# A graph layer with attention, a mixer and eight experts: the first nodes of the expert stage prepared in the last attention step, and the expert loop written out

## The reference

```python
xn = layernorm(x)
gnn = relu(gat_conv(xn))          # softmax over each node's edges, 4 heads of 64:
                                  #   out[n] = sum_e exp(e)*xp[src] / sum_e exp(e)
qkv = xn @ W_qkv + b_qkv          # q, k centred; q2 = l2norm(q*q / (sum q*q + 1e-7)) per node
mix = (v + q2 @ kv / sqrt(N)) @ W_out + b_out
x = x + gnn + mix                 # "base" of a node below: x + v-part + scaled q-part + constant
z = layernorm(x)
w = softmax(mean_over_batch(z) @ Wr + br)            # 8 weights a node
for e in range(8):                                   # three 256x256 products each
    h = relu(bn(z @ W1[e] + b1[e])); h = relu(bn(h @ W2[e] + b2[e]))
    x += w[:, e] * (h @ Wo[e] + bo[e])
```

## Time and profile before

| quantity | value |
|---|---|
| median of 3 runs | 3340.61 us (3336.39 to 3344.05) |
| the profiled execution: its own time | 3340.92 us |
| the profiled execution: span | 3339.1 us |
| PE busy | 2875.5 us (86%) |
| DVE busy | 2209.1 us (66%) |
| ACT busy | 1550.5 us (46%) |
| POOL busy | 1505.3 us (45%) |
| mean granted TensorE clock | 0.867 of full speed |
| `experts` stage, first instruction to end of span | 2214.04 to 3339.1 us |

### The profile page before, as it was taken

How to read it: one execution, slowest core, us unless ns; L and a number is a source line. 1 busy time by engine, 2 the same in 40 slices (tenths; PEclk the granted TensorE clock), 3 DMA queues, 4 the chain that set the end, 5 groups by cost and what they waited for, 6 DMA issues and landing times. The chain is left out here.

```text
span 3339.1 us, 62774 instructions
## 1 busy us (share of the span) xinstructions
PE 2875.5 (86%) x18549; PEld 2173.3 (65%) x18549; DVE 2209.1 (66%) x6073; ACT 1550.5 (46%) x4109; POOL 1505.3 (45%) x1625
## 2 busy tenths in 40 slices
PE   5678887888887888888888888859999999999999
PEld 3567666667766776777777777745665656566655
DVE  5457787787887877887878888864444444545424
ACT  3245555555555565565565555533332333333332
POOL 0177777777777777777777777500000000000000
PEclk9777888887877888787788787869999999999999
DMA  7544444444444444444444444431001010101000
GB/s 245 171 138 121 126 121 121 123 124 123 124 115 114 125 129 125 128 122 124 128 127 127 126 124 123 101 128 34 22 24 45 1 45 0 45 1 45 1 12 11
DMA packets 163365, 316.34 MB, mean 95 GB/s; under 512 B 32208, under 2 KB 97360, under 8 KB 162896
## 3 DMA queue, kind: packets, MB, share of 16 engines
q0 software_dynamic: 75552, 212.96, 24.5%
q1 hardware_dynamic: 78576, 90.49, 8.5%
q10 hardware_dynamic: 8896, 8.82, 0.8%
HBM read 272.44 MB, written 39.70 MB: 93 GB/s over the span
## 5 line engine op out<-in xcount | busy, mean ns | idle before, releaser
L758 POOL DMA_INDIRECT xg<-edge_table,idx x1568 | 1490.3, 950 | 501.7 <-issue 485.3
L1024 PE MATMUL ps_y<-y,hotw 128*128 128x260 f32 x3520 | 909.3, 421 | 41.0 <-issue 37.9
L1024 PEld LDWEIGHTS ps_y<-y,hotw 128*128 128x128 f32 x3520 | 721.9, 212 | 201.1 <-issue 50.8
L1515 ACT ACTIVATE h<-ps_h,bnb,bns 128x448 f32<-128x448 f32 x448 | 324.1, 723 | 624.2 <-PE ps_h L1475 624.2
L1617 DVE SCALAR_TENSOR_TENSOR yb<-ps_ye,wts,yb 128x256 f32<-128x256 f32 x392 | 189.7, 484 | 576.0 <-PE ps_ye L1483 576.0
L891 ACT ACTIVATE y<-xg,w 128x65 f32 x1760 | 466.5, 338 | 7.4 <-ACT w L883 0.4
L1241 DVE TENSOR_TENSOR y<-xg,ps_v 128x780 f32<-128x780 f32 x440 | 418.1, 961 | 8.8
L940 ACT CAST hotw<-hot 128x512 f32<-128x512 bf16 x440 | 267.1, 622 | 272.8 <-PE ps_y L1024 271.8
L1475 PE MATMUL ps_h<-zt,w 128*128 128x448 f32 x896 | 362.3, 559 | 6.0 <-issue 5.7
L1483 PE MATMUL ps_ye<-wo,h 128*128 128x256 f32 x1568 | 348.1, 379 | 0.0
L1475 PE MATMUL ps_h<-h,w 128*128 128x448 f32 x896 | 345.9, 539 | 0.0
(11 more groups left out here) (231 smaller groups left out, 2880.5 us busy)
## 6 DMA issues: line engine op xcount, KB each, us to landing
xg<-edge_table,idx POOLq DMA_INDIRECT x1568
mix_rows<-kk SPq DMA_DIRECT2D x49, 257.0 KB
t<-mix_rows SPq DMA_DIRECT2D x7, 1799.0 KB, 7.6
xb<-xn_turned SPq DMA_DIRECT2D x50, 128.0 KB
x<-in_x SPq DMA_DIRECT2D x7, 896.0 KB, 8.0
xn_rows<-xn SPq DMA_DIRECT2D x7, 896.0 KB, 5.1
xn_turned<-xnt SPq DMA_DIRECT2D x7, 896.0 KB, 8.5
x7e<-in_x SPq DMA_DIRECT2D x7, 896.0 KB, 9.7
```

Of the source, the lines that this page charges most:

```text
L758: pool.indirect_dma_start(xg[:, q * OCT + u, j, :], None, dr["table"], bass.IndirectOffsetOnAxis(ap=idx[q][:, c:c + 1], axis=0)).then_inc( ...
L1024: mm = pe.matmul(ps_y[v % 2][:, 0:RW], hotw[v % 2][:, j, :], y[v % 2][:, j, :], start=(j == 0), stop=(j == CH - 1))
L1515: act.activation((h1, h2)[layer][:, mh, half * HN:(half + 1) * HN], ps_h[g % 4][:, 0:HN], ACT.Relu, bias=K.bnb[:, layer, c:c + 1], scale=K ...
```

## The change

- The ring `xg` and the lists of the attention stage are no longer freed before `experts`: its buffers `t7`, `x7`, `yb`, `q7`, `zt`, `h2` are now places in the ring (`t7`, `x7` and `yb[0]` in its upper half), and `h1` lies over three index tables. Rows of the kernel after therefore name these tiles `xg` and `tables`.
- In the last attention step SP waits until the step before has been read out of the ring and then loads `t7` and `x7` of the first group. ACT takes the root after its second visit, DVE does the six tiny operations after adding up its second visit (`first_scales`), and POOL adds up the base in four passes over all seven blocks (128x1792 numbers each): one as soon as the loads have landed, three after DVE's sixth operation.
- The first group has a way of its own in `experts` (`first_nodes`, `turns`, `turned`): three operations a block on DVE in place of six, statistics and normalisation for four blocks and then for three, PE transposes four blocks, does the first half of the first expert's first layer, transposes three, and goes on. The router's products come after the first expert's hidden layers.
- SP issues the weights first, and `bo` behind the second expert's.
- The hardware loop is gone; all seven groups are written out.
- The last group is stored in two DMAs, four blocks and three.
- `attend` has five counting semaphores more, `experts` three.

```diff
+                pool.wait_ge(first_in, 32)
+                pool.tensor_tensor(K.yb[0], K.t7[:, :, D + 2:MW], K.x7, ALU.add).then_inc(base_d, 1)
+                pool.wait_ge(fq3_d, ONE + 3)
+                pool.tensor_tensor(K.t7[:, :, 0:D], K.t7[:, :, 0:D], bc(small[:, 5, :], 2, D), ALU.mult).then_inc(base_d, 1)
+                pool.wait_ge(base_d, ONE + 2)
+                pool.tensor_tensor(K.yb[0], K.yb[0], K.t7[:, :, 0:D], ALU.add).then_inc(base_d, 1)
+                pool.wait_ge(base_d, ONE + 3)
+                pool.tensor_tensor(K.yb[0], K.yb[0], bc(K.cb[:], 1, IB), ALU.add).then_inc(base_d, 1)
...
+                    if n(1) == FREE:
+                        sp.wait_ge(mix_out, 16 + 16 * IB)
+                        sp.wait_ge(y_d, ONE + FREE * SV)
+                        sp.wait_ge(ya_d, ONE + FREE * SV)
+                        sp.dma_start(K.t7, dr["mix"][0:IN_, :].rearrange("(j p) c -> p j c", p=P)).then_inc(first_in, 16)
+                        sp.dma_start(K.x7, io["x"][0:IN_, :].rearrange("(j p) c -> p j c", p=P)).then_inc(first_in, 16)
...
+                        if v == 1 and n(1) == NS - 1:
+                            act.wait_ge(first_in, 32)
+                            act.activation(small[:, 2, :].unsqueeze(2), K.t7[:, :, D + 1:D + 2], ACT.Sqrt).then_inc(froot_d, 1)
...
+                        if v == 2 and n(1) == NS - 1:
+                            first_scales()
...
-            with eng.Fori(0, NI // 2) as i:
-                for q in range(2):
-                    iteration(q, lambda c, q=q, i=i: i * (2 * c) + q * c, True)
-            iteration(0, lambda c: (NI - 1) * c, False)
+            for g in range(NI):
+                q, more = g % 2, g + 1 < NI
+                t = lambda c, g=g: g * c
...
+                        last = t(1) == NI - 1
+                        for lo, hi in ((0, HALF), (HALF, IB)) if last else ((0, IB),):
+                            sp.wait_ge(S["expert_added"], ONE + t(E * IB) + (E - 1) * IB + hi)
...
+                            if first and layer == 0:
+                                if half == 1:
+                                    turns(q, t, HALF, IB)
+                                pe.wait_ge(S["node_reads"], ONE + (IB if half else HALF))
...
+                    if first:
+                        for k, at in enumerate((slice(0, HALF), slice(HALF, IB))):
+                            act.wait_ge(S["half_var"], ONE + k + 1)
+                            act.activation(small[:, 9, at], small[:, 8, at], ACT.Sqrt).then_inc(S["half_std"], 1)
+                            if k == 0:
+                                turned(q, t, 0, HALF)
...
+                    for j in range(IB):
+                        gat(j, t)
+                        dve.wait_ge(S["gat_done"], ONE + j + 1)
+                        dve.scalar_tensor_tensor(yb[q][:, j, :], q7[:, j, :], 0.0, yb[q][:, j, :], ALU.max, ALU.add).then_inc(S["z_done"], 1)
+                        dve.wait_ge(S["z_done"], ONE + j + 1)
+                        dve.bn_stats(stats[:, j, :], yb[q][:, j, :]).then_inc(S["stats_done_e"], 1)
+                        if j == HALF - 1:
+                            half_var(0, 0, HALF)
+                        if j == HALF:
+                            half_norm(0, 0, HALF)
+                    half_var(1, HALF, IB)
+                    half_norm(1, HALF, IB)
```

More of the change, by code:

```diff
@@ L1364, in experts @@
         wo = m.sb("wo", [P, 2, E, D])
[L1365 to L1371, removed]
+        h1, h2, zt, yb, x7, q7, t7 = K.h1, K.h2, K.zt, K.yb, K.x7, K.q7, K.t7
         bo = m.sb("bo", [P, E, D])
@@ L1423, in node @@
-                        if not before:
-                            sp.dma_start(bo[:].rearrange("p e d -> p (e d)"),
-                                         io["b_o"].rearrange("e d -> (e d)").partition_broadcast(P)).then_inc(bo_in, 16)
-                            for e in range(E):
-                                for dst, name in ((w1, "w1"), (w2, "w2"), (wo, "wo")):
-                                    sp.dma_start(dst[:, :, e, :], io[name][:, :, e, :]).then_inc(w_in[e], 16)
+                        sp.wait_ge(S["z_done"], ONE + before(IB) + IB)
@@ new lines, in expert @@
+                        if not last:
+                            sp.wait_ge(out_d, t(16) + 16)
+                            sp.sem_inc(S["stored"], 1)
+                for e in range(E):
+                    for dst, name in ((w1, "w1"), (w2, "w2"), (wo, "wo")):
+                        sp.dma_start(dst[:, :, e, :], io[name][:, :, e, :]).then_inc(w_in[e], 16)
+                    if e == 1:
+                        sp.dma_start(bo[:].rearrange("p e d -> p (e d)"),
+                                     io["b_o"].rearrange("e d -> (e d)").partition_broadcast(P)).then_inc(bo_in, 16)
@@ L1458, in node, with turns @@
                         mm.then_inc(S["node_products"], 1)
+                def turns(q, t, lo, hi):
+                    for j in range(lo, hi):
+                        pe.wait_ge(S["node_reads"], ONE + t(NPR) + (j if j == 0 else j - 1))
+                        pe.wait_ge(S["zn_done"], ONE + t(IB) + (j + 1))
+                        for kh in range(2):
+                            mm = pe.transpose(ps_n[j % 2][:, kh * P:(kh + 1) * P], x7[:, j, kh * P:(kh + 1) * P], ident)
+                        mm.then_inc(S["node_products"], 1)
                 def expert(e, q, t):
-                    if e == 0:
+                    first = e == 0 and t(1) == 0
+                    if first:
+                        turns(q, t, 0, HALF)
+                    elif e == 0:
                         pe.wait_ge(S["node_reads"], ONE + t(NPR) + NPR)
@@ L1505, in node, with turned @@
                         act.activation(lg[:], lg[:], ACT.Exp).then_inc(S["lg_exp"], 1)
+                def turned(q, t, lo, hi):
+                    for j in range(lo, hi):
+                        product(3, j, t)
+                        act.copy(zt[q][:, :, j * P:(j + 1) * P], ps_n[j % 2][:, 0:D].rearrange("p (k n) -> p k n", n=P)).then_inc(S["node_reads"], 1)
                 def expert(e, q, t):
                     done = t(E * HB) + (e * HB)
+                    first = e == 0 and t(1) == 0
+                    if first:
+                        for k, at in enumerate((slice(0, HALF), slice(HALF, IB))):
[3 more added lines that the diff above has]
+                                turned(q, t, 0, HALF)
                     for layer in range(2):
                         for half in range(2):
+                            if first and layer == 0 and half == 1:
+                                turned(q, t, HALF, IB)
                             for mh in range(2):
@@ L1608, in expert @@
                 def expert(e, q, t):
+                    if e == 0 and t(1) == 0:
+                        first_nodes(q, t)
+                        node(4, q, t, None)
                     if e == 0:
```

137 lines of the change are left out of this document (91 added, 46 removed).

## The result

| | before | after |
|---|---|---|
| median of 5 runs | 3342.19 us (3336.39 to 3345.73) | 3322.38 us (3319.85 to 3326.58) |
| the profiled execution: own time, span | 3340.92, 3339.1 us | 3326.58, 3324.8 us |
| mean granted TensorE clock | 0.867 | 0.871 |

The ratio is 0.994 (95% interval 0.9928 to 0.9952), a gain of 19.8 us where 23 were forecast. That the sum came out near hides two errors of its terms that partly cancel: the end of the attention stage became some 10 us dearer than forecast, the start of the experts 6 us cheaper.

A forecast was written before the change was run, and what follows sets the result against it. Waits and DVE work before the experts' first matmul (39.6 us), then PE alone, bound the kernel. -17.3 (start), -10.5 + 2.4 (loop), -1.4 (store), +3.0 (passes), +0.8 (semaphores) = -23.0: 3318 us, range 3311 to 3327.

The forecast's parts named there:

- the end of the attention stage: Last attention step and turn to the experts: POOL's late passes +3.0 us, eight more counting semaphores +0.8.
- the start of the experts: Expert stage's start until the first expert's hidden layers and router are done: less waiting and DVE work, -17.3 us.
- The loop and the output layers: Expert groups written out: two back-edge pauses and slow layers behind them go, -10.5 us; dearer output layers, +2.4.
- The last store: End of the program: 512 KB of the 896 KB store leave three blocks earlier, -1.4 us.
- The six operations: DVE's tiny operations moved into the last attention step: 1.26 us there, DVE's end at 2211.6 at most.
- the eight semaphores: Eight more counting semaphores to raise at 0.1 us each, +0.8 us.
- The price of a pass on POOL: Last attention step: each POOL pass over 1792 numbers taken as 4.0 us, bounded above by 12.4.
- Rival 1: Last attention step: POOL's first pass holds up DVE near 2185, all later by 3.4 us, 3321; chance 0.30.
- I take 4.0 and 0.1 between passes: end at 2213.3, +3.0: End of attention: POOL's three late passes start at 2201.03 and end the stage at 2213.3, +3.0 us.
- I carry that over: clock up at 9.1 + 16.8 = 25.9: Expert stage's start: PE's clock rises 16.8 us after its first work, as before, at 25.9 us.
- the dip: First group: the clock falls after the router as in later groups, costing 1.8 us.
- wait for the softmax: First group: PE waits about 0.5 us for the softmax after its first two products.

The follow-up runs named there:

- e13_warm_short: 16 filler PE products at the expert stage's start, added to the kernel with early drain, held first pass and early semaphores; ratio 0.9911 to the kernel before.
- e12_warm: 30 filler PE products at the expert stage's start, added to the kernel with early drain, held first pass and early semaphores; 3311.83 us, ratio 0.9908.

## Why the prediction was right, step by step

**Right in size.** The loop and the output layers (-8.1 predicted; the loop alone -6.7 in the trace and -7.1 in the medians), where a layer became 0.06 us dearer on the mean in place of 0.05, and the rest of the difference is within the scatter of the falling clock. The last store (-1.4; -1.6 in the trace, 1.5 in the kernel with one store). The six operations (about 1 us, at most 1.3 predicted) and the eight semaphores (0.5 us for five and 0.2 for three, 0.8 predicted). The price of a pass on POOL, 4.0 us taken, is 3.19 to 3.74. By the figure of the Trainium skill (GPSIMD Engine Reference, section 3.1), about 2.6 cycles an element, an estimate for a two-input pass is 3.9 us; all four here are below it.

**Rival 1 was what happened.** The forecast left it out, so here a rival's mechanism was right and the forecast's wrong. POOL's first pass held up DVE by 3.44 us (3.62 in place of 0.18); the prediction had priced this at 3.4 and given it 0.30. Its ground against, that a few tens of ns are no standstill, was wrong: the rows on the cast came from POOL's short indirect issues and said nothing of a 3.6 us pass. The kernels without a first pass at that time have no hold; in those with it there is one of 3.37 to 3.62 us each time, on whichever of four operations DVE had reached. The Trainium skill (SBUF — State Buffer, "Who interferes with whom") has it that a DVE operation with two SBUF inputs and a GpSimd one that reads SBUF exclude each other for a whole instruction; by that rule the trace agrees, 3.62 and 3.44 us against passes of 3.61.

**The term that failed: "I take 4.0 and 0.1 between passes: end at 2213.3, +3.0".** It took the end of POOL's last pass for the end of the stage. In fact the passes ended with DVE and cost nothing by themselves; what they did was to stand between the gathers and the drain, so that 9.2 us which had been covered since 2152.2 came to lie on the path: +9.4 in the turn. Moved ahead of the passes, the drain left a turn of 3.99. The row had been in the trace of before, among the queue's rows, and was not read: only POOL's compute rows were. The measured end of attention is +14.1 (4.65 and 9.4) where +3.8 stood.

**The step that gave it back: "I carry that over: clock up at 9.1 + 16.8 = 25.9".** Measured from PE's first work it was 6.6 us, not 16.8. The one row of before had short router products between transposes and hidden layers, and with those put back the clock again stayed low for 18.9 us. Counted from the first hidden-layer product the rise came after 5.8 us before the change, 5.6 with the router first, 3.9 in the changed kernel, and 2.0 to 3.3 in other traces with the changed kernel's order: what the engine is given to do mattered more than the time since it started, but neither count gives the moment. Together with a start 1.0 us earlier this ends the hidden layers 4.8 us sooner than forecast; the dip that didn't come in this trace, and a longer wait for the softmax against it, give the other 1.4 of the 6.3 us.

So the forecast was right in sign and near in size, by the loop and the store as argued, and because +10.2 and -6.3 partly cancelled. That they did was luck. With rival 1 and its own other terms it would have said 3321.

## What to carry to other kernels

Before work is appended to a GpSimd list that ends in a barrier, look at the drain behind its last software DMA: 9.2 us are free there as long as others work, and on the path once GpSimd is made the last. Issue a drain, and the semaphores of the next stage, in that free time. When a wait of a clock is carried over from a trace, carry it from the same kind of work, not from the start of the stage. And before a difference of a few microseconds is put down to an edit, look in both traces at how often the clock fell in the part that the edit leaves alone.

## What the hardware showed that I had not expected

- POOL's DRAIN behind indirect DMAs: 9.206 us in every trace where it follows the gathers directly, though their transfers had landed, and 9.3 us beyond the last pass where the passes stand between; 9.5 to 10.0 in `prepare`, where it begins before the last indirect DMA is issued; 0.034 to 0.041 in the blocks where no indirect DMA has been issued since the last drain. What it does in that time no row tells.
- DVE stands for what is left of a whole POOL instruction: one operation of 0.18 to 0.23 us took 3.37 to 3.62, in five traces.
- Raising 37 semaphores by POOL took 3.2 us, 0.09 each, and with the block around it 3.7.
- After 7.1 us of filler products the clock stayed up over pauses of 0.84 and 0.64 us and fell within the router's 28 short products (e13_warm_short); in e12_warm it did not fall there.
- Behind the routers of the later groups the clock falls in some executions of a kernel and not in others, and that moves its time by about 5 us.
